# The first product of a feed-forward in seven block products instead of eight, for two batches at a time

## The chip, the cores and the metric

The kernel runs on one core of a Trainium2 chip. The metric is the device time of one execution in microseconds (us), the median of the runs shown. The engines are TensorE (PE, and PEld for its weight loads), VectorE (DVE), ScalarE (ACT), GpSimd (POOL) and the queue of SyncE (SP), which issues nearly every DMA.

## The reference

Four batches, each of 512 tokens with 512 features, pass through one block with cross attention (16 heads of 32 features):

```python
x = layer_norm(hidden_states, ln1_w, ln1_b)
q, k, v = x @ q_w + q_b, ctx @ k_w + k_b, ctx @ v_w + v_b     # split into 16 heads
out = softmax(q k^T / sqrt(32) + mask) v
hidden = out @ cproj_w + cproj_b + hidden_states
y = layer_norm(hidden, ln2_w, ln2_b)
y = gelu(y @ fc_w + fc_b)                                     # 512 -> 2048
return hidden + y @ proj_w + proj_b                           # 2048 -> 512
```

The change is to the line with `fc_w`. Everything is float32.

## The kernel before, in words

A product in float32 is formed as three passes of TensorE on `float32r` operands. Each operand is split into a high part (a rounded copy) and a low part (operand minus high part), and `mm3` (lines 487 to 489) issues high by high, low by high and high by low into one bank of PSUM. So each operand costs one copy and one subtraction of its size on some engine before TensorE can use it.

Stages: projections; attention, a loop of 64 steps i (16 head groups s, four key blocks kc each); then the feed-forward, a loop of NJ = 64 steps i, with b = i // 16 the batch and f = i % 16 the slab of 128 hidden features. `fc(i)` forms hidden features f of batch b for its 512 tokens: four blocks of 128 input features, 12 matmuls of 128x512, into bank 4 or 5. ScalarE's `gelu(i)` (line 832) reads the bank, VectorE splits the result into the tile HR (line 1178 the copy, line 1180 the subtraction), and `pj(i)` multiplies it with `proj_w`: 12 matmuls that accumulate into banks 0 to 3 through the 16 steps of a batch. TensorE's order is fc(i), pj(i-1), so that the GELU and the split of a step have a whole product to hide behind. Steps 2 to 5 also hold `cproj(3, c)`, the attention's output projection for the last batch, 12 matmuls each.

Weights are loaded once: `load_slab(f)` brings 256 KB of `fc_w` and 256 KB of `proj_w` into the raw tile RW; `slab_high` and `slab_low` (line 838 on ScalarE or 1066 on VectorE, lines 1221 or 1044 for the low part) split them, and all 16 slabs then stay in SBUF for the four batches. From step 12 on nothing of the weights is loaded or split.

The second layer norm of batch b+1 runs beside the steps of batch b: `ln2_load`, `statistics` (line 932), `aggregate`, `root` on GpSimd (line 1226), `norm` (945), a transpose through DRAM (`y_block` 960, `y_store` 345, `y_load` 352), `y_affine` (964), `y_high` on ScalarE (849) and `y_low` on GpSimd (1221). At the end of a batch VectorE adds the banks to the residual (`add`, line 1190), SP stores them (455), reloads the tile with the next batch's residual (477), and GpSimd adds the bias (1349, four instructions a batch).

Each engine works its own list in program order. A wait of one instruction holds all behind it on that engine. The order is written out by hand, engine by engine, and semaphores tie the lists together. In attention, VectorE's or GpSimd's `pair_add` (lines 1038, 1325) adds pairs of exponentials, `sums(15)` on TensorE (625) needs the last of them, and `divide_a` to `divide_c` with `split_out(15)` and `out_low(15)` lead from it to `cproj(3, c)`.

## Time and profile before

| | |
|---|---|
| median of 3 runs | 771.24 us (770.92 to 771.43) |
| the profiled execution, first to last instruction | 769.3 us |
| its own time | not given apart; the median stands 1.9 us above its span |
| granted TensorE clock | 0.999 of full |
| busy: PE, DVE, ACT, POOL | 744.1, 457.1, 281.4, 299.1 us |
| DMA | 103.25 MB, mean 134 GB/s |

A matmul's start is measured and its end is modelled, so its listed length overlaps the next one's; the pace of TensorE is read from start to start.

### The profile page before, as it was taken

The page shows a single profiled execution, that of the slowest core. Times are in us where ns is not written, and L with a number is a line of the kernel's source. Part 1 is how long each engine was busy: PE and PEld are TensorE (multiplying, and loading weights), DVE is VectorE, ACT ScalarE, POOL GpSimd, SP SyncE. Part 2 cuts the span into 40 slices and gives each one's busy share as a digit, 9 for nine tenths or more (in the row PEclk, how much of TensorE's full clock was granted, in tenths as well). Part 3 has the DMA queues.
Part 4 walks back from the last instruction along what each step waited for, and adds up shares of the span by engine and source line. Part 5 has one row for each costly group of instructions (what it writes and reads, how often), then busy time and mean ns, then how long its engine had stood idle before and what let it go on. Part 6 is the DMA issues. An engine that isn't in the chain of part 4 may idle for free.

```text
span 769.3 us, 10036 instructions
## 1 busy us (share of the span) xinstructions
PE 744.1 (97%) x3664; PEld 514.2 (67%) x3664; DVE 457.1 (59%) x995; ACT 281.4 (37%) x492; POOL 299.1 (39%) x183
## 2 busy tenths in 40 slices
PE   7999999989999999999999999999999999999998
PEld 5878886733344444444436888888888888888886
DVE  6673347778888888898697668443424333232213
ACT  4534241276766566667682011211112111211110
POOL 2654150068998778798754002212002200220000
PEclk9999999999999999999999999999999999999999
DMA  9656377597666785678641537240220413030001
GB/s 328 231 167 214 136 220 240 193 268 167 158 164 146 184 216 145 156 209 177 176 136 53 181 109 202 74 165 0 42 69 18 147 18 93 1 109 1 1 0 55
DMA packets 94385, 103.25 MB, mean 134 GB/s; under 512 B 39968, under 2 KB 48420, under 8 KB 94336
## 3 DMA queue, kind: packets, MB, share of 16 engines
q1 hardware_dynamic: 94192, 102.59, 46.5%
q8 instruction: 29, 0.48, 0.2%
q14 instruction: 20, 0.16, 0.1%
q10 hardware_dynamic: 144, 0.02, 0.0%
HBM read 73.08 MB, written 29.37 MB: 133 GB/s over the span
## 4 chain that ended last, share of the span: by engine, by line
PE 80%; DVE 12%; issue 3%; ACT 2%; DMA 1%; POOL 1%; SPq 0%; ACTq 0%; DVEq 0%
PE ps L487 22%; PE ps L488 21%; PE ps L489 21%; DVE ps L1009 6%; PE ps L594 4%; PE ps L610 4%; PE ps L579 4%; PE ps L625 3%; DVE R L1144 2%; ACT Pt L797 1%; PE ps L547 1%; DVE mx L1009 1%; DMA qs<-BIG 1%; DVE R L945 1%; DVE st L932 1%
## 5 line engine op out<-in xcount | busy, mean ns | idle before, releaser
L797 ACT ACTIVATE Pt<-ps 128x512 f32<-128x512 f32 x256 | 137.6, 598 | 70.9 <-PE ps L594 69.6
L1178 DVE CAST HR<-R 128x512 fp32r<-128x512 f32 x52 | 24.9, 478 | 186.0 <-ACT R L832 186.0
L832 ACT ACTIVATE R<-ps,cols 128x512 f32<-128x512 f32 x52 | 35.9, 690 | 227.2 <-PE ps L489 227.1
L594 PE MATMUL ps<-BIG 98*128 98x512 f32 x256 | 93.2, 439 | 3.6 <-ACT Pt L797 3.2
L1009 DVE CUSTOM_DVE_ANT_0 ps<-ps,FU 128x512 f32<-128x512 f32 x128 | 84.6, 724 | 14.9 <-PE ps L579 14.8
L1009 DVE CUSTOM_DVE_ANT_0 ps<-ps,BIG 128x512 f32<-128x512 f32 x128 | 84.6, 723 | 10.8 <-PE ps L579 10.7
L594 PEld LDWEIGHTS ps<-BIG 98*128 98x128 f32 x256 | 44.2, 187 | 68.3 <-issue 29.3
L487 PE MATMUL ps<-BIG,HR 128*128 128x512 f32 x192 | 74.8, 390 | 1.0 <-DVE HR L1180 1.0
L487 PE MATMUL ps<-YT,BIG 128*128 128x512 f32 x192 | 74.9, 390 | 0.0
L488 PE MATMUL ps<-YT,BIG 128*128 128x512 f32 x192 | 74.7, 389 | 0.0
L489 PE MATMUL ps<-BIG,HR 128*128 128x512 f32 x192 | 74.7, 389 | 0.0
L489 PE MATMUL ps<-YT,BIG 128*128 128x512 f32 x192 | 74.7, 389 | 0.0
L488 PE MATMUL ps<-BIG,HR 128*128 128x512 f32 x192 | 74.7, 389 | 0.0
L610 PE MATMUL ps<-Pt,V 128*32 128x512 f32 x512 | 68.2, 605 | 0.0
L1325 POOL TENSOR_TENSOR R<-Pt 128x1024 f32<-128x1024 f32 x20 | 47.3, 2388 | 45.9 <-ACT Pt L797 45.9
L1221 POOL TENSOR_TENSOR BIG<-R,BIG 128x512 fp32r<-128x512 f32 (+1 forms) x31 | 42.2, 1388 | 42.1 <-ACT BIG L809 22.8
L487 PE MATMUL ps<-BIG 128*128 128x512 f32 x128 | 52.8, 413 | 5.8 <-DVE BIG L1077 5.8
L1221 POOL TENSOR_TENSOR YT<-R,YT 128x512 fp32r<-128x512 f32 x12 | 15.5, 1308 | 109.1 <-ACT YT L849 109.1
L1325 POOL TENSOR_TENSOR RAWY<-Pt 128x1024 f32<-128x1024 f32 x22 | 52.0, 2385 | 4.8 <-ACT Pt L797 4.8
L488 PE MATMUL ps<-BIG 128*128 128x512 f32 x128 | 50.9, 398 | 0.0
L487 PE MATMUL ps<-BIG,WK 128*128 128x512 f32 x128 | 50.8, 397 | 0.0
L489 PE MATMUL ps<-BIG 128*128 128x512 f32 x128 | 50.7, 396 | 0.0
(132 smaller groups left out, 1371.3 us busy)
## 6 DMA issues: line engine op xcount, KB each, us to landing
BIG<-qs SPq DMA_DIRECT2D x62, 256.0 KB, 2.8
BIG<-ks SPq DMA_DIRECT2D x62, 256.0 KB, 3.2
ks<-BIG SPq DMA_DIRECT2D x32, 256.0 KB, 2.0
qs<-BIG SPq DMA_DIRECT2D x32, 256.0 KB, 5.8
R<-hd SPq DMA_DIRECT2D x28, 256.0 KB, 3.9
R<-in_x SPq DMA_DIRECT2D x16, 256.0 KB, 5.4
hd<-R SPq DMA_DIRECT2D x16, 256.0 KB, 3.2
yt<-FU SPq DMA_DIRECT2D x64, 64.0 KB, 1.9
```

The source lines that it names most:

```text
L487: eng.matmul(outp, a[0], b[0], start=first, stop=False)
L488: eng.matmul(outp, a[1], b[0], start=False, stop=False)
L489: return eng.matmul(outp, a[0], b[1], start=False, stop=last)
L579: eng.matmul(bank(bank_b(RB[("s1", 4 * group + j)])), lead(s)[r, 0, qc * 128:(qc + 1) * 128], lead(s)[r, 1, :], start=True, stop=True).the ...
L594: eng.matmul(bk, K_[0:98, j, kc * 128:(kc + 1) * 128], Q_[0:98, j, :], start=True, stop=True).then_inc(S["p_ra"], 1)
L610: ins = eng.matmul(bank(7)[32 * j:32 * j + 32, :], V[:, 4 * b + kc, c:c + 32], Pt[:, r, j % 2, :], start=kc == 0, stop=kc == 3)
L797: eng.activation(Pt[:, r, j % 2, :], bank(bank_a(("s2", i, j))), ACT.Exp, scale=SCALE).then_inc(S["a_ra"], 1)
L832: eng.activation(g, bank(4 + i % 2), ACT.Gelu_apprx_tanh, bias=fcb[:, f:f + 1]).then_inc(S["a_g"], 1)
L1009: eng.tensor_tensor_reduce(out=scores, in0=scores, in1=MASK[s // 4], scale=1.0, scalar=-3.4e38, op0=ALU.add, op1=ALU.max, accum_out=mx[:, ...
L1178: eng.tensor_copy(HR[:, n, 0, :], g).then_inc(S["v_hh"], 1)
L1221: eng.tensor_tensor(dst, src, high.bitcast(F32), ALU.subtract).then_inc(S[name], 1)
L1325: eng.tensor_tensor(pair(m)[:, 2 * hp:2 * hp + 2, :], Pt[:, (r - 2) % 6, :, :], Pt[:, r, :, :], ALU.add).then_inc(S["g_ac"], 1)
```

## The change

Take two batches, q = 0 or 1 for the pair (2q, 2q+1). Let A be `fc_w` in 2 x 2 blocks (input features halved, hidden features halved) and B the normalised input in 2 x 2 blocks (features halved, the two batches side by side). The 2 x 2 block product takes eight block products; the Winograd form of Strassen's takes seven, with four sums of blocks of A, four of B, and more additions of results. A block product for one slab index p (0 to 7, HF = 8) is `product`: two blocks of 128 input features, 6 matmuls. So a slab pair (p, p+8) for two batches takes 42 matmuls where it took 48; `pj` keeps its 12 a step.

Each pair q now has three phases. **Front** (`fc_first`, `fc_second`, p = 0 to 7): product 1 is formed and copied out by ScalarE (`copy_first`), product 2 accumulates onto it in the bank, and the GELU follows. **Rest**: products 6, 5, 7, 4, 3 for each p, in two banks; VectorE adds between them (`add_u2`, `add_u3`, `add_c22`, `add_c21`, `add_c12`), and products 7, 4 and 3 wait for `add_u2`, `add_u3` and `add_c22`. **Second product**: 32 steps `pj(n)`, back to back. The hidden features of a pair are held in SBUF (`hidden`). The sums of weight blocks are formed on GpSimd (`weight_sums`, four instructions of 128x256 into one buffer SUMS), copied on ScalarE (`rest_high`, 256 then 1024 columns) and subtracted on VectorE (`rest_low`). The sums of input blocks are formed on VectorE (`blocks`, four of 128x1024), copied on ScalarE (`block_high`, five) and subtracted on VectorE (n = 0, 1) and GpSimd (n = 2, 3, 4). Weights are loaded and split again for each pair of batches, in 112 loads of 256 KB through a ring of four. The core of the diff:

```diff
+        SUMS = FU.rearrange("p a n -> p (a n)")
...
+        RAW_W = []
+        for q in range(2):
+            RAW_W += [("wf", HF * q + p, p) for p in range(HF)]
+            for p in range(HF):
+                RAW_W += [("wr", HF * q + p, p), ("wr", HF * q + p, p + HF)]
+            RAW_W += [("pj", NF * b + f, f) for b in (2 * q, 2 * q + 1) for f in range(NF)]
...
+        def raw_done(n):
+            kind, m, _ = RAW_W[n]
+            if kind == "wf":
+                return front_low(m)
+            return ("v_wr", 2 * m + 2) if kind == "wr" else ("g_pj", m + 1)
...
+            def store_out(b):
+                for c in range(4):
+                    sp.wait_ge("v_o", 4 * b + c + 1)
+                    eng.dma_start(ov[4 * b + c], R2[:, c, :]).then_inc(S[f"d_o{c}"], 16)
...
+                            if n == 8 + c:
+                                y_store(2, c)
+                            if n == 17 + c:
+                                y_store(3, c)
+                        if n == 12:
+                            y_load(2)
+                        if n == 21:
+                            y_load(3)
+                    if n == 18:
+                        store_out(2 * q)
+                        residual(2 * q + 1)
...
+                for k in ks:
+                    ins = mm3(outp, [x[:, 128 * k:128 * k + 128] for x in a], [y[:, k - ks[0], :] for y in b],
+                              first and k == ks[0], k == ks[-1], onto=not first)
+                return ins
...
+            def fc_first(q, p):
+                m = HF * q + p
...
+                pe.wait_ge(*front_low(m))
+                pe.wait_ge("a_yp", 4 * q + 2)
+                pe.wait_ge("g_yp", 4 * q + 2)
+                product(bank(FRONT_BANKS[q][p % 4]), front(q, p), [YT0[:, h, 0:2, :] for h in range(2)], (0, 1),
+                        True).then_inc(S["p_p1"], 1)
...
+            def fc_second(q, p):
+                m = HF * q + p
...
+                product(bank(FRONT_BANKS[q][p % 4]), front(q, p), [YT0[:, h, 2:4, :] for h in range(2)], (2, 3),
+                        False).then_inc(S["p_p2"], 1)
...
+            def fc_rest(q, p, which):
+                m = HF * q + p
+                b, c = (bank(FRONT_BANKS[q][(2 * p + j) % 4]) for j in range(2))
+                outp, a, y, done = {6: (b, 2, 1, "p_p6"), 5: (c, 1, 0, "p_p5"), 7: (b, 3, 2, "p_p7"),
+                                    4: (b, 0, 3, "p_p4"), 3: (c, 4, 4, "p_p3")}[which]
+                pe.wait_ge("v_wr", 2 * m + 2)
+                pe.wait_ge("a_yq", 5 * q + y + 1)
+                pe.wait_ge(*(("v_yq", 2 * q + y + 1) if y < 2 else ("g_yq", 3 * q + y - 1)))
+                if which in (6, 5):
+                    if p < 2:
+                        pe.wait_ge("a_g11", HF * q + 5 + 2 * p + (which == 5))
+                    else:
+                        pe.wait_ge(*(("v_c21", m - 1) if which == 6 else ("v_c12", m - 1)))
+                elif which == 7:
+                    pe.wait_ge("v_u2", m + 1)
+                elif which == 4:
+                    pe.wait_ge("v_u3", m + 1)
+                else:
+                    pe.wait_ge("v_c22", m + 1)
+                product(outp, [x[:, 256 * a:256 * a + 256] for x in rest(p)], YQ[y], (0, 1),
+                        which in (6, 5)).then_inc(S[done], 1)
...
+            def pj(n):
+                b, f = divmod(n, NF)
+                sl = second(n)
+                pe.wait_ge("v_hl", n + 1)
+                pe.wait_ge("g_pj", n + 1)
...
+            for q in range(2):
+                fc_first(q, 0)
+                for p in range(HF):
+                    if p + 1 < HF:
+                        fc_first(q, p + 1)
...
+                    fc_second(q, p)
...
+                for which in (6, 5, 7):
+                    fc_rest(q, 0, which)
+                for p in range(HF):
+                    if p + 1 < HF:
+                        fc_rest(q, p + 1, 6)
+                    fc_rest(q, p, 4)
+                    if p + 1 < HF:
+                        fc_rest(q, p + 1, 5)
+                    fc_rest(q, p, 3)
+                    if p + 1 < HF:
+                        fc_rest(q, p + 1, 7)
+                for n in range(32 * q, 32 * q + 32):
+                    pj(n)
...
+            def rest_high(q, p):
+                m = HF * q + p
+                n = RAW_AT[("wr", m, p + HF)]
...
+                else:
+                    act.wait_ge("p_p2", 2 * HF)
+                    act.wait_ge("p_pr", 128)
+                hi = rest(p)[0]
+                eng.activation(hi[:, 0:256], raw_w(n)[:, 256:512], ACT.Copy).then_inc(S["a_wr"], 1)
+                act.wait_ge("g_s", 4 * m + 4)
+                eng.activation(hi[:, 256:1280], SUMS, ACT.Copy).then_inc(S["a_wr"], 1)
...
+            def second_high(n):
...
+                    act.wait_ge("p_pr", 4 * (n - 2))
+                eng.activation(second(n)[0], raw_w(at), ACT.Copy).then_inc(S["a_pj"], 1)
...
+            for q in range(2):
...
+                for p in range(HF):
+                    if p + 1 < HF:
+                        copy_first(q, p + 1)
+                    gelu11(q, p)
...
+                    if q == 0 and p == 6:
+                        for n in range(4):
+                            block_high(0, n)
+                    if p == 6 and q:
+                        rest_high(q, 0)
+                if q == 0:
+                    block_high(0, 4)
+                    rest_high(q, 0)
+                rest_high(q, 1)
+                gelu_rest(q, 0, 22)
+                rest_high(q, 2)
+                for p in range(HF):
+                    gelu_rest(q, p, 21)
+                    gelu_rest(q, p, 12)
+                    if p + 3 < HF:
+                        rest_high(q, p + 3)
+                    if p == 5:
+                        for n in range(3):
+                            second_high(32 * q + n)
+                    if p + 1 < HF:
+                        gelu_rest(q, p + 1, 22)
+                for n in range(32 * q, 32 * q + 32):
+                    if n + 3 < 32 * q + 32:
+                        second_high(n + 3)
+                    if q == 0:
+                        if n == 16:
+                            for k in range(4):
+                                y_high(2, k)
+                        if n == 26:
+                            for j in range(4):
+                                block_high(1, j)
+                            block_high(1, 4)
+                        if 28 <= n:
+                            front_high(1, n - 28)
...
+            def rest_low(q, p):
+                m = HF * q + p
+                hi, lo = rest(p)
+                dve.wait_ge("a_wr", 2 * m + 1)
+                eng.tensor_tensor(lo[:, 0:256], raw_w(RAW_AT[("wr", m, p + HF)])[:, 256:512], hi[:, 0:256].bitcast(F32),
+                                  ALU.subtract).then_inc(S["v_wr"], 1)
+                dve.wait_ge("a_wr", 2 * m + 2)
+                eng.tensor_tensor(lo[:, 256:1280], SUMS, hi[:, 256:1280].bitcast(F32), ALU.subtract).then_inc(S["v_wr"], 1)
...
+                for n, a, b in ((0, b2[:, 0:2, :], b1[:, 0:2, :]), (1, b2[:, 2:4, :], formed(q, 0)),
+                                (2, b2[:, 2:4, :], b2[:, 0:2, :]), (3, b1[:, 2:4, :], formed(q, 1))):
+                    if n in (1, 3):
+                        dve.wait_ge("v_tt", 4 * q + (1 if n == 1 else 2))
+                    eng.tensor_tensor(formed(q, n), a, b, ALU.subtract).then_inc(S["v_tt"], 1)
...
+            def add_u2(q, p):
...
+            def add_u3(q, p):
+                m = HF * q + p
...
+                eng.tensor_tensor(hidden(1, p + HF), bank(FRONT_BANKS[q][2 * p % 4]), hidden(0, p + HF), ALU.add).then_inc(S["v_u3"], 1)
...
+            for q in range(2):
+                for p in range(HF):
...
+                    if q == 0 and p == 5:
+                        blocks(0)
+                    if q == 0 and p == 6:
+                        block_low(0, 0)
+                        block_low(0, 1)
+                rest_low(q, 0)
+                add_u2(q, 0)
+                rest_low(q, 1)
+                add_u3(q, 0)
+                add_c22(q, 0)
+                for p in range(HF):
+                    if p + 1 < HF:
+                        add_u2(q, p + 1)
+                    add_c21(q, p)
+                    add_c12(q, p)
+                    if p + 2 < HF:
+                        rest_low(q, p + 2)
+                    if p + 1 < HF:
+                        add_u3(q, p + 1)
+                        add_c22(q, p + 1)
+                    if p >= HF - 2:
+                        split_hidden(32 * q + p - HF + 2)
+                for n in range(32):
+                    m = 32 * q + n
+                    if n >= 2:
+                        split_hidden(m)
+                    if n == 17:
+                        add_out(2 * q)
+                    if q == 0:
...
+                            if n - at == 7:
+                                for c in range(4):
+                                    norm(LN[b], b % 2, 4 + b, c)
...
+                            if 14 <= n - at < 16:
+                                for k in (2 * (n - at) - 28, 2 * (n - at) - 27):
+                                    y_affine(b, k)
+                        if n == 25:
+                            blocks(1)
+                        if n == 27:
+                            block_low(1, 0)
+                            block_low(1, 1)
+                        if 28 <= n:
+                            front_low_part(1, n - 28)
...
+            def block_low(q, n):
...
+            def weight_sums(q, p):
...
+                pool.wait_ge(*raw_come(n1))
...
+                a1, a2 = raw_w(n1), raw_w(n2)
+                s1, s2, s3, s4 = (SUMS[:, 256 * j:256 * j + 256] for j in range(4))
+                eng.tensor_tensor(s1, a2[:, 0:256], a2[:, 256:512], ALU.add).then_inc(S["g_s"], 1)
+                eng.tensor_tensor(s3, a1[:, 0:256], a2[:, 0:256], ALU.subtract).then_inc(S["g_s"], 1)
+                pool.wait_ge("g_s", 4 * m + 1)
+                eng.tensor_tensor(s2, s1, a1[:, 0:256], ALU.subtract).then_inc(S["g_s"], 1)
+                pool.wait_ge("g_s", 4 * m + 3)
+                eng.tensor_tensor(s4, a1[:, 256:512], s2, ALU.subtract).then_inc(S["g_s"], 1)
...
+            def second_low(n):
+                pool.wait_ge("a_pj", n + 1)
...
+            def bias_add(b):
+                pool.wait_ge("d_pb", 16)
+                for c in range(4):
+                    pool.wait_ge(f"d_hb{c}", 16 * (b + 1))
+                    eng.tensor_tensor(R2[:, c, :], R2[:, c, :], cbt[:, :], ALU.add).then_inc(S["g_hb"], 1)
...
+            for q in range(2):
+                weight_sums(q, 0)
+                if q == 0:
+                    for n in (2, 3, 4):
+                        block_low(0, n)
+                else:
+                    bias_add(2)
+                for p in range(HF):
+                    if p + 1 < HF:
+                        weight_sums(q, p + 1)
+                    if q == 0 and p == 2:
+                        bias_add(0)
+                    if p == HF - 1:
+                        for n in range(3):
+                            second_low(32 * q + n)
+                for n in range(32):
+                    m = 32 * q + n
+                    if n + 3 < 32:
+                        second_low(m + 3)
+                    if n == 21:
+                        bias_add(2 * q + 1)
+                    if q == 0:
+                        if n == 6:
+                            root(0, 6)
+                        if n == 15:
+                            root(1, 7)
+                        if n == 17:
+                            for k in range(4):
+                                y_low(2, k)
+                        if n == 27:
+                            for j in (2, 3, 4):
+                                block_low(1, j)
```

## Rows read from the trace of the kernel before

**Rows 1.** The page: busy time, share of the span and instructions by engine.
```profile
PE 744.1 (97%) x3664; PEld 514.2 (67%) x3664; DVE 457.1 (59%) x995; ACT 281.4 (37%) x492; POOL 299.1 (39%) x183
```

**Rows 2.** Feed-forward, windows: us; busy PE, PEld, DVE, ACT, POOL; clock, DMA share, GB/s.
```profile
403.30:764.80 361.50, 360.47 (x1596) 296.81 (x1597) 152.97 (x270) 54.24 (x81) 49.55 (x37) 1.00 0.23 68
```

**Rows 3.** PE's timeline: start, length, line, form [idle before <-releaser].
```profile
417.52 0.50 PE L487 MATMUL ps<-BIG,HR 128*128 128x512 f32 x1 [1.03 <-DVE HR L1180]
...
420.39 0.39 PE L487 MATMUL ps<-BIG 128*128 128x512 f32 x1
...
431.27 0.39 PE L487 MATMUL ps<-YT,BIG 128*128 128x512 f32 x1
```

**Rows 4.** Groups from 420 us on: xcount | busy us, mean ns of one.
```profile
L1180 DVE TENSOR_TENSOR HR<-R,HR 128x512 fp32r<-128x512 f32 x52 | 38.0, 730 | 1.8
L832 ACT ACTIVATE R<-ps,cols 128x512 f32<-128x512 f32 x52 | 35.9, 690 | 227.2 <-PE ps L489 227.1
...
L1178 DVE CAST HR<-R 128x512 fp32r<-128x512 f32 x52 | 24.9, 478 | 186.0 <-ACT R L832 186.0
L1349 POOL TENSOR_TENSOR R<-R,cbt 128x512 f32<-128x512 f32 x16 | 21.7, 1387 | 64.8 <-DMA R<-hd 64.8
...
L1190 DVE TENSOR_TENSOR R<-ps,R 128x512 f32<-128x512 f32 x16 | 10.2, 684 | 1.5 <-PE ps L489 1.5
...
L945 DVE TENSOR_SCALAR R<-R,mv,rs 128x512 f32<-128x512 f32 x12 | 6.5, 541 | 0.0
```

**Rows 5.** Groups of ACT over the whole run.
```profile
L757 ACT ACTIVATE BIG<-RAWY 128x1024 fp32r<-128x1024 f32 x4 | 4.0, 1049 | 0.0
```

**Rows 6.** Groups of POOL over the whole run.
```profile
L1221 POOL TENSOR_TENSOR BIG<-R,BIG 128x512 fp32r<-128x512 f32 x29 | 37.5, 1316 | 28.3 <-ACT BIG L809 22.8 <-ACT BIG L763 5.5
...
L1221 POOL TENSOR_TENSOR BIG<-RAWY,BIG 128x1024 fp32r<-128x1024 f32 x4 | 9.7, 2448 | 18.1 <-ACT BIG L757 18.1
...
L1226 POOL TENSOR_TENSOR rs<-ve,mh 128x4 f32<-128x4 f32 x8 | 8.5, 1059 | 74.1 <-DVE ve L941 74.1
```

**Rows 7.** Line 1038, DVE's sums of 128x1024: duration ns min/median/max.
```profile
L1038 DVE TENSOR_TENSOR V<-Pt x6: 1212/2068/2301, 378.7 to 402.9; 128x1024 f32<-128x1024 f32 x6
```

**Rows 8.** DVE's timeline.
```profile
389.40 4.52 DVE L1038 TENSOR_TENSOR V<-Pt 128x1024 f32<-128x1024 f32 x2
...
401.20 2.90 DVE L1038 TENSOR_TENSOR V<-Pt 128x1024 f32<-128x1024 f32 x2 [0.45 <-ACT Pt L797]
...
473.00 1.27 DVE L1178 CAST HR<-HN 128x512 fp32r<-128x512 f32 x1 [1.21 <-ACT HN L832]
```

**Rows 9.** POOL's timeline.
```profile
389.07 8.21 POOL L1221 TENSOR_TENSOR YT<-HN,YT 128x512 fp32r<-128x512 f32 x4 [1.47 <-ACT YT L849]
...
471.44 5.69 POOL L1349 TENSOR_TENSOR R<-R,cbt 128x512 f32<-128x512 f32 x4 [18.54 <-DMA R<-hd]
```

**Rows 10.** DMA issues: xcount, KB each, median us from issue to landing.
```profile
yt<-FU SPq DMA_DIRECT2D x64, 64.0 KB, 1.9
RW<-in_fc_w SPq DMA_DIRECT2D x16, 256.0 KB, 3.3
...
R<-yt SPq DMA_DIRECT2D x12, 256.0 KB, 4.2
```

**Rows 11.** SP's timeline: the time its queue takes to issue.
```profile
480.07 1.75 SPq L352 DMA_DIRECT2D R<-yt  x4
...
764.71 2.37 SPq L455 DMA_DIRECT2D out<-R  x4
```

**Rows 12.** PE's first matmuls.
```profile
5.75 0.76 PE L487 MATMUL ps<-BIG 128*128 128x512 f32 x1 [5.75 <-DVE BIG L1077]
...
9.73 0.63 PE L487 MATMUL ps<-BIG 128*128 128x512 f32 x1
...
10.77 0.39 PE L487 MATMUL ps<-BIG 128*128 128x512 f32 x1
```

**Rows 13.** The stretch after the last matmul, in the columns of rows 2.
```profile
766.00:769.00 3.00, 0.00 (x0) 0.00 (x0) 0.73 (x2) 0.00 (x0) 0.00 (x0) 0.87 0.78 292
```

586 lines of the change are left out of this document (358 added, 228 removed).

## The prediction

> **What bounds the kernel now.** I read the page first, for busy shares: TensorE is busy 744.1 of 769.3 us, the others under 60% [rows 1]. Then the view of windows, cut to the feed-forward: PE 360.47 of 361.50 us, while DVE works 153.0, ACT 54.2, POOL 49.6 [rows 2]. So TensorE alone sets this stage's end, and every matmul taken out there is worth its time as long as nothing else makes TensorE wait. Then PE's own timeline, for the pace and the gaps: from 420.39 to 431.27 us it starts 48 matmuls, 10.88/48 = 0.2267 us each, and the only gap in the stage is 1.03 us at its start [rows 3]. The listed 0.39 us are not the pace. A step of 12 matmuls is 2.72 us, a block product of 6 is 1.36 us.
>
> The sum is made against the profiled span of 769.3 us; the median of the runs, 771.24, stands 1.9 above it, and I carry that over. A measurement of this kernel can tell about 0.2%, 1.5 us, from no change.
>
> **What is removed.** 64 x 12 = 768 first-product matmuls become 16 x 42 = 672. 96 x 0.2267 = **-21.8 us**, all of it on the path.
>
> **What is added** is work for engines that had room on average, placed where TensorE may have to wait for it. The durations: a split of a hidden tile on DVE is a copy of 0.41 and a subtraction of 0.69 alone, means 0.48 and 0.73; a GELU 0.69; a PSUM addition 0.68; a bias addition on POOL 1.39; one `norm` 0.54 [rows 4]. A copy of 128x1024 on ACT is 1.05 [rows 5]. On POOL 128x512 is 1.32 and 128x1024 is 2.45, so 1.13 for 512 columns; 128x256 isn't in the trace, its bounds are the smallest instruction, 1.06, and a line through the two, 0.75 [rows 6]. I take 0.75, since 256 columns lie on that line, and keep the other for the range. DVE's 128x1024 sum is 1.21 alone [rows 7]; its 128x256 I put at 0.4 by the same reasoning.
>
> **DVE and POOL together.** DVE's 128x1024 sums at 389.4 take 2.26 each, not 1.21, while POOL's four subtractions beside them take 2.05 each, not 1.3 [rows 8, 9]. At 473.0 copy and subtraction take 1.27 and 1.67 beside POOL's bias additions [rows 8, 9]. Each engine seems to wait for the other's instruction to end. That speaks against this change, which puts POOL beside DVE throughout. The Trainium skill says so (SBUF — State Buffer, Who interferes with whom): the second port pair is an exclusive lock, held for a whole instruction, taken by a DVE instruction with two SBUF inputs or in a two-port mode. Under that rule every DVE split queues behind a POOL instruction; without it DVE's durations would stay at the short ones. The trace agrees with the rule.
>
> *Start of the stage, q = 0.* Four `statistics` and the aggregates go ahead of the last pair sums on DVE, some 2.5 to 3 us, where it had 0.45 us to spare [rows 8]; the removed `slab_high(2)`/`slab_low(2)` came only after those. `cproj(3,0)` then waits for the quotient's chain through ACT and POOL. The gap of 1.03 us goes [rows 3]. Between 0 and 3 net, I take **+1**.
>
> *Front to rest, q = 0.* Product 6 needs `block_high`, `rest_high(0)` and `rest_low(0)`. ACT's list puts four blocks behind GELU 6 and a fifth behind GELU 7. From the end of `fc_second(6)`: 0.69 + 4 x 1.05 + 0.69 + 1.05 + 0.3 + 1.05 on ACT, then 1.21 on DVE = 9.2 us. TensorE has one product, 1.36, to do meanwhile: 7.8 us idle. POOL's three `block_low` of 2.45 lie there too, the last one just ahead of DVE's `rest_low`, which costs up to 2.5 more. After the start, 6(1) needs the chain again: sums 4 x 0.75, copy 1.05, subtraction 1.21 = 5.3 us against three products, 4.1: 1.2 more. 9 to 13, I take **+11.5**.
>
> *Front to rest, q = 1.* `rest_high` waits for the last front product (its buffer overlays `front`): 0.3 + 1.05 + 1.21 + 0.2 = 2.8, and the same 1.2. **+4** (3 to 5).
>
> *The clock.* After 5.75 us without work TensorE's first matmuls start 0.427 us apart until about 10.5 us, then 0.227 (rates of 1.2 and 2.4 GHz) [rows 12]; and in the 3 us after the last matmul the granted clock averages 0.87 [rows 13]. So the idle 11 us should drop the clock: 11 matmuls x 0.2 = 2.2 us, partly inside the 1.2 above. **+1** (0 to 4).
>
> *Rest, steady.* Five products are 6.80 us. But a loop closes through DVE: `add_c12`, `rest_low(p+2)` (0.3 + 1.13 by spacing), `add_u3`, then products 4, 5, 3: 0.19 (from a product's last start plus 0.23 to its modelled end, and to DVE's start) + 0.6 + 0.3 + 1.13 + 0.69 + 0.05 + 4.2 = 7.16. 0.36 x 14 = **+5** (0 to 8, the top if POOL's sums take 1.06). `bias_add(0)` stands among them: 4 x 1.39 on POOL, beside `rest_low`: **+1.5** (0 to 2.5). The two loads of the next slab, 3.3 us to landing [rows 10], have a period of 7; covered.
>
> *Second product, q = 0.* The period is 2.72; a split has 1.6 us of slack. (a) n = 7 and 14 to 18: `norm` x4, affine x4, `add_out` (2.7) and `y_low` x4 pile up on DVE and POOL: 0 if they don't share, 4.7 if they do. (b) SP, n = 17 to 21: four stores (2.37), the residual's wait and loads, the transposes' stores (2.0 each), then `y_load(3)` (1.75 to issue, 4.2 to land) [rows 10, 11]: `y_affine(3)`, ahead of the split of n = 24 on DVE, starts 3.3 to 5 us late, and the raw `proj_w` tiles come late too. (c) n = 25: `blocks(1)`, 4 x 1.13 after a split of 1.1, against 2.72 + 1.6: 2.1 to 4.6. (d) n = 27: DVE's `block_low` waits for ACT's `block_high(1,0)`, which waits for `pj(26)`'s end; the split of n = 28 stands behind: 0.65 + 2 x 1.05 + 1.2 + 1.1 = 5.1 against 2.72: 2.5. (e) POOL does three `block_low` (7.3) before the low part for n = 31: ready 15.8 us after `pj(26)` against 13.4: 2.4, and 5.1 with DVE's splits in between. Together 10.3 to 21.9, I take **+14.5**. *q = 1* has only the bias additions at n = 21: **+1** (0.3 to 1.8).
>
> *Costed at nothing:* the front's copies and GELUs (1.9 of 2.72 us on ACT), the low parts of `proj_w` (POOL 1.3 of 2.72), the 112 loads (one of 256 KB in 2.72 us is 96 GB/s, below the run's mean of 134). Their cover is TensorE's own period; if it were gone, POOL's 64 low parts would be the next thing late.
>
> Sum: -21.8 + 1 + 11.5 + 4 + 1 + 5 + 1.5 + 14.5 + 1 = **+17.7**; 771.2 + 17.7 = **789.0**.
>
> **Rivals.** (R1) DVE and POOL don't disturb each other much and the side work fits: the low ends, 0 + 9 + 3 + 0 + 3 + 0 + 10.3 + 0.3 = 25.6, less 21.8: 775. Against it stand [rows 8, 9]. (R2) Faster. Its place is the second product of q = 0: if DVE's and SP's extra work there costs under 5 us rather than 14.5, and the steady rest nothing, 11.5 + 4 + 1 + 2 = 18.5 against 21.8: 768. It decides at 21.8 us of TensorE waits in all. For it: DVE is idle over half of this stage [rows 2], and one late split is soon made up. Against it: the two hand-overs alone take some 13 of it. (R3) The chain POOL, ACT, DVE sets the rest's period: POOL's sums at 1.06 to 1.32 each make 4.2 to 5.3 + 2.3 + waits = 7.5 to 8, 0.5 more for 14 periods and 2 more at each hand-over: 800. (R4) Terms cancel within 1.5 us.
>
> **How the numbers follow.** Forecast, 780 to 797: 0.57. R1: 0.13. R2: 0.13. R3: 0.12. R4: 0.05. So faster 0.13, same 0.05, slower 0.82. The range leaves out R2 and R4's lower half and the far end of R3: 773 to 802; the forecast's own terms, all at their ends, give 772 to 804.
>
> **What would show it.** Right: 96 matmuls fewer at an unchanged 0.227 us; a PE gap of 8 to 12 us before the first product 6 of q = 0, ended by DVE's `rest_low`, and of about 3 for q = 1; starts 0.427 apart behind the long gap; rest periods near 7.2; DVE splits of 1.2 to 3 us beside POOL's instructions; gaps in the second product of q = 0 ended by the split or by POOL's low part. Wrong: a stage without PE gaps of several us; a matmul pace that changes; DVE's durations as short as alone; or the second product of q = 0 at 32 x 2.72 = 87 us.

## The result: 831.6 us, 60 above the kernel before

The changed kernel takes 831.62 us (median of 4, 830.73 to 833.20) against 771.34 (770.92 to 771.72) for the kernel before in the same session: a ratio of 1.0786, 95% interval 1.0772 to 1.0799. Slower, as forecast, but by 60 us where I had 18, and 30 us above the top of my range. The profiled spans are 831.4 and 769.3 us, so 62 us are to be found.

The page of the kernel after, its busy shares, and the strips of 40 slices of PE and of the clock:

```profile
span 831.4 us, 10419 instructions
PE 747.7 (90%) x3568; PEld 505.1 (61%) x3568; DVE 546.7 (66%) x1077; ACT 362.2 (44%) x618; POOL 448.3 (54%) x307
PE   7999999989999999999995888987775988899998
PEclk9999999999999999999997999989977989999999
```

The matmuls are 96 fewer, yet PE is busier than before [rows 1], 747.7 for 744.1: some of what is left ran slower. PE's strip is broken from the 22nd slice on, and only there does the clock's strip fall to 7 or 8, in five slices. The view of windows, cut at the stages (columns as in [rows 2]; the last three figures are the granted clock, the DMA share and GB/s):

```profile
430.00:450.00 20.00, 10.94 (x46) 8.71 (x45) 15.09 (x14) 9.44 (x13) 13.65 (x7) 0.82 0.57 170
450.00:520.00 70.00, 61.28 (x248) 47.86 (x247) 41.29 (x58) 26.97 (x40) 30.21 (x36) 0.95 0.32 102
520.00:620.00 100.00, 79.95 (x314) 62.90 (x313) 69.50 (x103) 18.52 (x30) 52.85 (x36) 0.90 0.47 132
620.00:650.00 30.00, 20.64 (x75) 16.11 (x75) 15.64 (x18) 9.31 (x13) 11.35 (x6) 0.82 0.30 96
650.00:720.00 70.00, 62.77 (x259) 49.73 (x258) 31.64 (x46) 31.32 (x49) 26.11 (x34) 0.95 0.25 76
720.00:831.00 111.00, 104.39 (x454) 84.42 (x452) 57.33 (x87) 27.14 (x42) 58.20 (x40) 1.00 0.34 105
```

Before, PE was busy nearly all of this stage [rows 2]. Now no engine is full in the broken windows: DVE, the busiest beside PE, has 15.1 of 20 us in the first and 69.5 of 100 us in the third. PE waits, for work that is late rather than for an engine that is full. The waits, from PE's timeline (distances of two starts less 0.227 us): hand-over of the first half 9.22 and 1.36; steady rest 13 of 1.05 or 0.94 and one of 2.43; its second product 4.54, 4.26, 6.73, 3.08, 2.84, 6.85 and three smaller ones (0.68, 0.39, 1.48), 30.9 in all; hand-over of the second half 2.91; its second product 2.5. With 2.7 at the stage's start that is 65.5 us. Besides, 78 matmuls in nine stretches, each behind a wait of 2.43 us or more, start late after the one before them, nearly all 0.427 us instead of 0.227 (the first of a stretch often 0.59): 16.6 us more than at 0.227.

**The hand-over.** PE's timeline around the longest wait; the bracket names the idle time and what ended it:

```profile
439.54 0.39 PE L590 MATMUL ps<-YT,RX 128*128 128x512 f32 x1
448.99 0.80 PE L588 MATMUL ps<-SLX,BIG 128*128 128x512 f32 x1 [9.06 <-DVE BIG L1322]
449.58 0.63 PE L589 MATMUL ps<-SLX,BIG 128*128 128x512 f32 x1
```

And what DVE, POOL and ACT did before it, from their timelines:

```profile
440.81 2.34 DVE L1339 TENSOR_TENSOR SLX<-BF,SLX 128x1024 fp32r<-128x1024 f32 x2
...
445.88 3.06 DVE L1322 TENSOR_TENSOR BIG<-FU,BIG 128x1024 fp32r<-128x1024 f32 x1 [0.23 <-ACT BIG L1047]
445.33 5.82 POOL L1595 TENSOR_TENSOR YT<-BF,YT 128x1024 fp32r<-128x1024 f32 x2
444.80 1.05 ACT L1047 ACTIVATE BIG<-FU 128x1024 fp32r<-128x1024 f32 x1
```

`rest_low` (L1322) takes 3.06 us, 1.21 alone, beside POOL's `block_low` (L1595). It starts when ACT's copy (L1047) is done, at 445.8; so of the 9.2 us of waiting about 1.9 are the stretching, and the rest is the way to that copy.

**The rest, steady.** DVE's, ACT's and PE's timelines at the start of one product 6:

```profile
489.11 0.69 DVE L1381 TENSOR_TENSOR BF<-ps,BF 128x512 f32<-128x512 f32 x1 [2.03 <-PE ps L590]
489.72 0.42 DVE L1319 TENSOR_TENSOR BIG<-RW,BIG 128x256 fp32r<-128x256 f32 x1
490.05 1.22 DVE L1322 TENSOR_TENSOR BIG<-FU,BIG 128x1024 fp32r<-128x1024 f32 x1
486.43 1.06 ACT L1047 ACTIVATE BIG<-FU 128x1024 fp32r<-128x1024 f32 x1 [3.55 <-POOL FU L1661]
491.32 0.50 PE L588 MATMUL ps<-SLX,BIG 128*128 128x512 f32 x1 [0.90 <-DVE BIG L1322]
```

ACT had the high part ready at 487.49. DVE waited for product 3 to do `add_c12` first (L1381), then `rest_low(p+2)`, and PE, which has only product 7 to do meanwhile, waited for that: 0.2 + 0.6 + 0.3 + 1.2 = 2.3 us against 1.36, so some 1.0; 1.05 came.

**The second product of the first half.** Three of its waits, each with what DVE or POOL did (timelines; L1391 and L1393 are the copy and the subtraction of the split, L1214 is `norm`, L1600 `root`, L1233 `y_affine`, L1672 `bias_add`, L1595 at 630.78 and 633.10 `block_low`, L1313 `front_low`):

```profile
539.31 1.02 POOL L1600 TENSOR_TENSOR rs<-ve,mh 128x4 f32<-128x4 f32 x1
540.36 2.87 DVE L1214 TENSOR_SCALAR HN<-HN,mv,rs 128x512 f32<-128x512 f32 x4 [4.57 <-POOL rs L1600]
544.35 0.79 PE L588 MATMUL ps<-BIG,HR 128*128 128x512 f32 x1 [4.38 <-DVE HR L1393]
...
598.53 5.31 POOL L1672 TENSOR_TENSOR R<-R,cbt 128x512 f32<-128x512 f32 x4
600.71 2.02 DVE L1233 TENSOR_SCALAR R<-R,cols 128x512 f32<-128x512 f32 x2 [4.48 <-DMA R<-yt]
602.64 1.48 DVE L1391 CAST HR<-BF 128x512 fp32r<-128x512 f32 x1
604.16 1.64 DVE L1393 TENSOR_TENSOR HR<-BF,HR 128x512 fp32r<-128x512 f32 x1
605.85 0.79 PE L588 MATMUL ps<-BIG,HR 128*128 128x512 f32 x1 [6.57 <-DVE HR L1393]
...
630.78 2.35 POOL L1595 TENSOR_TENSOR YT<-BF,YT 128x1024 fp32r<-128x1024 f32 x1
633.10 2.78 POOL L1595 TENSOR_TENSOR YT<-R,YT 128x1024 fp32r<-128x1024 f32 x1
632.48 1.20 DVE L1313 TENSOR_TENSOR RX<-RW,RX 128x512 fp32r<-128x512 f32 x1 [5.94 <-ACT RX L1031]
633.60 2.56 DVE L1391 CAST HR<-BF 128x512 fp32r<-128x512 f32 x1
636.20 1.63 DVE L1393 TENSOR_TENSOR HR<-BF,HR 128x512 fp32r<-128x512 f32 x1
637.88 0.79 PE L588 MATMUL ps<-BIG,HR 128*128 128x512 f32 x1 [6.68 <-DVE HR L1393]
```

All three read alike: DVE is idle for 4.5 to 6 us, since the next instruction of its list, a piece of work for the next half, still waits, and the split that PE needs stands behind it. In the second and the third the split itself is stretched as well, beside POOL's `bias_add` and then its `block_low`: by 3.1 us in the third (2.56 and 1.63 for 0.41 and 0.69 alone).

### The profile page after: what moved, and what is told of

Read it like the earlier page. It is cut to its first block, busy times and chain, and to the rows that moved or that the text cites. A ratio compares the mean times of both kernels' runs of the same rounds, so it can differ in the third digit from the quotient of the medians.

```text
span 831.4 us, 10419 instructions
## 1 busy us (share of the span) xinstructions
PE 747.7 (90%) x3568; PEld 505.1 (61%) x3568; DVE 546.7 (66%) x1077; ACT 362.2 (44%) x618; POOL 448.3 (54%) x307
## 4 chain that ended last, share of the span: by engine, by line
PE 67%; DVE 19%; issue 4%; POOL 4%; ACT 3%; DMA 2%; SPq 2%; ACTq 0%; DVEq 0%
PE ps L588 18%; PE ps L590 17%; PE ps L589 17%; DVE ps L1278 5%; PE ps L711 4%; PE ps L695 4%; PE ps L680 3%; PE ps L726 3%; DVE BIG L1322 2%; DVE R L1481 2%; DVE R L1214 1%; POOL BIG L1595 1%; DVE HR L1391 1%; SPq L410 1%; DVE BF L1381 1%
## 5 line engine op out<-in xcount | busy, mean ns | idle before, releaser
L1595 POOL TENSOR_TENSOR BIG<-RW,BIG 128x512 fp32r<-128x512 f32 x66 | 101.5, 1542 | 112.7 <-ACT BIG L1057 110.9
L588 PE MATMUL ps<-BIG,HR 128*128 128x512 f32 x256 | 105.7, 413 | 31.5 <-DVE HR L1393 28.8
L1057 ACT ACTIVATE BIG<-RW 128x512 fp32r<-128x512 f32 x64 | 40.2, 631 | 154.8 <-PE ps L590 135.1
L590 PE MATMUL ps<-BIG,HR 128*128 128x512 f32 x256 | 103.5, 404 | 0.0
L589 PE MATMUL ps<-BIG,HR 128*128 128x512 f32 x256 | 103.3, 404 | 0.0
L588 PEld LDWEIGHTS ps<-BIG,HR 128*128 128x128 f32 x256 | 50.6, 198 | 47.4 <-DVE HR L1393 33.4
L1391 DVE CAST HR<-BF 128x512 fp32r<-128x512 f32 x64 | 37.2, 582 | 55.9 <-PE ps L590 55.8
L1595 POOL TENSOR_TENSOR BIG<-R,BIG 128x512 fp32r<-128x512 f32 (+1 forms) x31 | 42.4, 1395 | 43.5 <-ACT BIG L968 24.4
L588 PE MATMUL ps<-SLX,BIG 128*128 128x512 f32 x96 | 41.7, 435 | 25.1 <-DVE BIG L1322 25.1
L1656 POOL TENSOR_TENSOR FU<-RW 128x256 f32<-128x256 f32 x16 | 11.8, 740 | 95.9 <-DVE BIG L1322 59.5
L588 PE MATMUL ps<-BIG 128*128 128x512 f32 x128 | 52.7, 412 | 6.1 <-DVE BIG L1410 5.8
L589 PEld LDWEIGHTS ps<-BIG,HR 128*128 128x128 f32 x256 | 50.9, 199 | 10.5
L590 PEld LDWEIGHTS ps<-BIG,HR 128*128 128x128 f32 x256 | 50.2, 196 | 11.2
L1393 DVE TENSOR_TENSOR HR<-BF,HR 128x512 fp32r<-128x512 f32 x64 | 53.9, 843 | 2.2
```

What stands on the lines that cost most here:

```text
L588: eng.matmul(outp, a[0], b[0], start=first, stop=False, skip_group_check=onto)
L589: eng.matmul(outp, a[1], b[0], start=False, stop=False, skip_group_check=onto)
L590: return eng.matmul(outp, a[0], b[1], start=False, stop=last, skip_group_check=onto)
L1057: eng.activation(second(n)[0], raw_w(at), ACT.Copy).then_inc(S["a_pj"], 1)
L1391: eng.tensor_copy(HR[:, n % 2, 0, :], g).then_inc(S["v_hh"], 1)
L1393: eng.tensor_tensor(HR[:, n % 2, 1, :], g, HR[:, n % 2, 0, :].bitcast(F32), ALU.subtract).then_inc(S["v_hl"], 1)
```

## The experiments

The theory after this: the saving of 21.8 us is real and in full; against it stand waits of PE, each made by the place of one piece of side work in a list, and each long one brings slow matmuls. The rivals to it: the clock (a cause of its own), POOL's weight sums (the chain POOL, ACT, DVE as the rest's bound), and port time of DVE and POOL together, so that gaps would only move.

**1. `rest_low` ahead of `add_c12` (e1_low_before_c12).**

```diff
                     add_c21(q, p)
-                    add_c12(q, p)
                     if p + 2 < HF:
                         rest_low(q, p + 2)
+                    add_c12(q, p)
```

> The changed kernel (831.6 us) with one pair of instructions moved on VectorE: in the rest phase rest_low(p+2) stands ahead of add_c12(p). Theory: the 13 PE gaps of 0.94 to 1.06 us, one a period, are there because product 6 of the next slab waits for rest_low, which waits in VectorE's list for product 3; they close, and with restarts 13 to 16 us go: 816 to 819. Rival: the chain of GpSimd's sums, ScalarE's copy and VectorE's subtraction sets the period of 7.99 us; then at most 3 us go: 828 or more.

Measured: 816.55 us (811.95 to 817.46), ratio 1.0577 (1.0548 to 1.0607), 15.1 less than the change. The same window of the steady rest, first in the kernel after, then here:

```profile
453.00:506.00 53.00, 45.96 (x189) 36.00 (x188) 30.90 (x43) 20.65 (x31) 23.36 (x30) 0.97 0.20 60
```

```profile
453.00:506.00 53.00, 51.73 (x223) 41.97 (x223) 37.24 (x52) 25.30 (x38) 27.95 (x32) 0.99 0.38 121
```

34 matmuls more in the same 53 us: all waits of 1.05 are gone, and so is the one of 2.43; one of 0.94 at the end of each rest stays. The time is the one expected (816 to 819). POOL's sums were not the bound.

**2. `root` one step earlier, ahead of `second_low` (e2_root_first).**

```diff
+                    if q == 0:
+                        if n == 5:
+                            root(0, 6)
+                        if n == 14:
+                            root(1, 7)
                     if n + 3 < 32:
                         second_low(m + 3)
...
                     if q == 0:
-                        if n == 6:
-                            root(0, 6)
-                        if n == 15:
-                            root(1, 7)
```

> The changed kernel with root(0,6) and root(1,7) on GpSimd one step earlier and ahead of second_low instead of behind it. Theory: the gaps of 4.54 and 4.26 us near 540 and 572 us come from norm waiting for root, which stands behind a second_low that waits for the end of a later pj; they close, and the slow matmuls behind them go too (2.2 + 1.6 us): 818 to 821. Rival: the norms stretched beside GpSimd (2.87 us for four) are what makes the split late; then the gaps keep 3 us or more each: 826 or more.

Measured: 824.73 us (822.18 to 826.55), ratio 1.0693. The waits of 4.54 and 4.26 shrink to about 1 each, so the cause is right; but only 7 us come, where 11 to 14 were expected: in the profile a later wait (6.85) grows to 8.44, another (3.08) to 3.84, and the hand-over's stands at 11.11, for 9.22. The edit does not touch that last one, so it scatters by some 2 us between runs.

**3. `rest_high(1,0)` one step earlier (e3_rest_high_early).** It now waits for the last user of its own buffer only.

```diff
-                    if p == 6 and q:
+                    if p == 5 and q:
                         rest_high(q, 0)
...
+                elif p == 0:
+                    act.wait_ge("p_p3", HF)
                 else:
                     act.wait_ge("p_p2", 2 * HF)
                     act.wait_ge("p_pr", 128)
```

> The changed kernel with rest_high(1,0) one step earlier on ScalarE and without its wait for the end of the front phase, since its buffer lies beside the front's. Theory: the gap of 2.91 us near 670 us goes, with the 13 slow matmuls behind it (2.6 us): 825 to 827. Rival: product 6 of slab 1 then waits as long, since its own chain starts late: 829 or more.

Measured: 829.32 us (828.95 to 830.75), ratio 1.0758. The wait of 2.91 at 669 us and its slow matmuls, 2.96, are gone, yet the time falls by 2.3, where 5 to 7 were expected and the rival had 3 at most. In the profile the rest of the second half has one more wait of 1.05, at 675 us, for slab 1, as the rival said, though far shorter than it had it; and the untouched first hand-over took 11.0 for 9.2.

**4. The price of a wait alone (gap5, gap2).** The kernel before, with PE made to wait six times, for five or for two small POOL instructions in a row; no other work changes.

```diff
+                if i in GAPS:
+                    pe.wait_ge("g_x", 5 * (GAPS.index(i) + 1))
```

(This is gap5; gap2 has 2 in place of 5.)

> The kernel before (771.3 us) with six waits put into TensorE's list, at steps 50, 52 and so on to 60: behind fc(i) it waits until GpSimd, which starts at fc(i)'s end, has done five instructions of 128x4 one after the other (about 1.0 us each by line 1226, so gaps near 5.3 us). If an idle stretch costs only itself: 6 x 5.3 = 32 us more, 803. If the clock falls in each and stays low for 8 to 10 matmuls, as behind the gaps of the changed kernel: 6 x (5.3 + 2.0) = 44, 815.

> As gap5, but two instructions on GpSimd per wait instead of five. By gap5's profile (6.24 us of gap for five, 1.24 each) the gaps are near 2.5 us: 15 us more than 771.1 if the clock holds (786), 29 more (800) if it falls behind each one.

Measured: gap5 823.75 us, ratio 1.0672 (1.0655 to 1.0690), 52.7 more than before; gap2 801.55, ratio 1.0383 (1.0349 to 1.0417), 30.6 more. PE's timeline of gap5 at its first wait, then of gap2 at its own:

```profile
697.15 0.80 PE L488 MATMUL ps<-BIG,HR 128*128 128x512 f32 x1 [6.08 <-POOL mx L1359]
697.74 0.63 PE L489 MATMUL ps<-BIG,HR 128*128 128x512 f32 x1
```

```profile
693.07 0.50 PE L488 MATMUL ps<-BIG,HR 128*128 128x512 f32 x1 [2.83 <-POOL mx L1359]
693.41 0.39 PE L489 MATMUL ps<-BIG,HR 128*128 128x512 f32 x1
...
694.67 0.63 PE L488 MATMUL ps<-BIG,HR 128*128 128x512 f32 x1
695.10 0.63 PE L489 MATMUL ps<-BIG,HR 128*128 128x512 f32 x1
```

In gap5 six waits of 6.24 (5.3 was expected) are 37.4, and 66 slow matmuls behind them cost 14.1: 51.5 of 52.7. In gap2 six of 2.98 are 17.9, and 55 slow matmuls 11.6: 29.5 of 30.6. So in these two runs a wait costs its length and some 2 us more, 1.4 to 3.0, whether it lasts 3 or 6 us. Nothing else was changed, so waits alone are enough to bring slow matmuls, and those of the changed kernel, each stretch behind a wait, need no cause of their own. Not every wait near 3 us brings them, though: behind 2.61 us in e2_root_first, and 2.90 in all1 and 2.92 in e5_second_spread (both below), the matmuls went on 0.23 us apart. PE's timeline of e5_second_spread:

```profile
656.72 0.50 PE L588 MATMUL ps<-SLX,BIG 128*128 128x512 f32 x1 [2.76 <-DVE BIG L1319]
657.05 0.39 PE L589 MATMUL ps<-SLX,BIG 128*128 128x512 f32 x1
657.29 0.40 PE L590 MATMUL ps<-SLX,BIG 128*128 128x512 f32 x1
```

**5. The order at the first hand-over (e4_handover).** ACT: `block_high(0,0)` a step earlier, `rest_high(0,0)` between blocks 1 and 2; POOL: `weight_sums(0,1)` between its `block_low` 2 and 3.

> The changed kernel with the hand-over from front to rest of q = 0 in another order: ScalarE does block_high(0,0) one step earlier, then block_high(0,1), rest_high(0,0) and block_high(0,2) ahead of the last GELU, and the other two blocks behind it; GpSimd does weight_sums(0,1) ahead of its last two block_low. Theory: rest_low(0) ends 4 to 6 us earlier, the gap of 9 to 11 us falls to 3.5 to 6 and the wait before product 6 of slab 1 grows to 2 to 3: 825 to 828. The clock still falls in the gap. Rival: the gap is set by GpSimd's and VectorE's turns with each other, not by ScalarE's list; then under 2 us go.

Measured: 832.13 us (828.63 to 835.34), ratio 1.0794: nothing. The first wait shrinks from 9.2 to 7.8, the next grows from 1.4 to 3.4 and now has slow matmuls of its own. ACT's copy was now ready at 441.0 instead of 445.8, and the first `rest_low` was not stretched either. DVE's timeline shows what bound instead:

```profile
441.08 4.50 DVE L1342 TENSOR_TENSOR SLX<-BF,SLX 128x1024 fp32r<-128x1024 f32 x2
...
445.83 1.21 DVE L1325 TENSOR_TENSOR BIG<-FU,BIG 128x1024 fp32r<-128x1024 f32 x1
```

That is DVE's own order: its two `block_low` (L1342), 4.50 us beside POOL's for 2.34 before, stand ahead of `rest_low`. The second `rest_low`, with POOL's last two `block_low` beside it, took 2.09 and 3.36, and that is the wait of 3.4.

**6. Side work spread out (e5_second_spread, on top of 2).** One `norm`, `y_high`, `y_low`, `blocks` and `block_low` a step instead of four at once; `bias_add(0)`, which stood in the rest, a row a step in the second product, those of batches 1 and 2 moved to the second half, that of batch 3 a row a step; SP's store and residual at n = 22 instead of 18, and `store_out(1)` and `add_out(1)` to step 3 of the second half's front.

> The changed kernel with the side work of q = 0's second product spread, one piece a step: root as in e2_root_first, norm, y_low, blocks and the block splits one a step, the bias additions of batches 0 and 3 one a step and of batches 1 and 2 moved to later, and SP's store_out(0) and residual(1) behind y_load(3). Theory: the gaps between 539 and 638 us (30.9 us in sum) with their slow matmuls (8 us) come from pieces in a lump ahead of a split; all but 5 us of them and the bias gap of 2.4 go: 831.6 - 33 = 795 to 802. Rival: GpSimd and VectorE together have no room there, whatever the order (GpSimd is busy 52.9 and VectorE 69.5 of 100 us); then at least 15 us of gaps stay: 810 or more.

Measured: 817.23 us (816.16 to 817.86), ratio 1.0599. That is above the 795 to 802 expected, and by its number in the rival's range. Up to 585 us the bundled waits become nine of 0.65 to 1.5 us, with hardly a slow matmul; but waits of 3.9 and 8.8 stay in its last steps. The count of instructions on DVE and POOL is the same over the run, so in those steps it was the bundling that made the long waits; the last steps this run does not settle.

**7. All five together (all1).**

> All edits of e1 to e5 together. Theory (the waits are separate, each closed by its own edit, and the clock falls only in gaps of over 2.4 us): 831.6 - 15 (e1) - 33 (e5 with e2) - 2.3 to 5 (e3) - 5 (e4) = 774 to 778, near the kernel before (771). If it falls under 771, the seven products pay once the waits are out. Rival: waits close only to open elsewhere: 785 or more.

Measured: 797.00 us (795.89 to 798.88), ratio 1.0341 (1.0325 to 1.0357): 34.6 off, some 20 less than hoped, and so in the range of the rival, that waits open elsewhere. 9.5 us of waits stand at the hand-over, and 8.88 at the end of the second product, where DVE's `front_low(1,0)` waits for ACT's `front_high(1,0)`, itself behind `second_high(31)`, which needs PE to go on.

**8. The order made again (all2).**

```diff
-                        if 28 <= n:
-                            front_low_part(1, n - 28)
+                        if n == 31:
+                            for p in range(4):
+                                front_low_part(1, p)
...
-                    for n in (2, 3, 4):
-                        block_low(0, n)
+                    weight_sums(0, 1)
+                    block_low(0, 4)
+                    block_low(0, 3)
```

(The first is DVE's list, the second POOL's; the rest is in the expectation. It isn't order alone: the `norm`s go to ACT and one `block_low` from POOL to DVE.)

> Everything of the run all1 except its order at the hand-over, and besides: (a) the second product of the first half: the four lows of the second half's front weights (0.68 each) stand behind the last split on DVE, so that no split waits for ACT's front_high; the norms of batches 2 and 3 (8 x 0.54 to 1.6) are made on ACT; bias_add(0) is spread over four rest periods; store_out(0) and residual(1) on SP stand five steps apart. (b) the hand-over of the first half: the second weight load of the first rest column goes out ahead of the y transpose's load, so POOL's weight sums can start some 5 us earlier; DVE makes three blocks, then block_low(1), rest_low(0), block_low(0) and block_low(2), and POOL makes weight_sums(1) ahead of its two block_lows, so that no POOL work lies beside rest_low(0). Theory (the time above the saving of 21.8 us is PE gaps made by the placing of side work, each gap above some 2.5 us with about 2 us of slow clock behind it): from all1's 797.0 the gaps of 8.88 (+2.36 slow), 2.69 (+1.51), 1.91, about 6.5 us of the gaps of 0.7, and 7 of the 9.5 at the hand-over (+1.96) go: 765 to 770. Rival 1, that the work is bound by the shared port of DVE and POOL and gaps only move: 785 or more, with the sum of gaps beyond 20 us. Rival 2, that the hand-over's chain is set by data (the y transpose lands at 431), not by order: a gap of 5 us or more stays there, 772 to 776.

Measured: 782.10 us (781.57 to 782.74), ratio 1.0137 (1.0114 to 1.0159). The time lies between the theory's 770 and the first rival's 785, above what the second had. The 8.88 is gone, the hand-over stands at 5.6 (1.19 and 4.42). But where POOL's `block_low` went, behind n = 28, waits of 2.47 and 3.29 came with a CAST of 2.57 and a subtraction of 2.73 on DVE: there the first rival was right, time of DVE and POOL beside each other had only moved.

**9. POOL's work beside DVE taken out (all3).** `weight_sums(0,1)`, all `block_low(0,·)` and `y_low(2)` on DVE, blocks 2 and 3 of the second half into its front, POOL's `block_low(1,·)` behind DVE's last split.

> On top of all2. Second product of the first half: y_low(2) moves from POOL to DVE (4 x 0.68 for 4 x 1.3 to 1.7), the block_lows 2 to 4 of the second half go out on POOL only behind the last split and its front lows, blocks 2 and 3 and block_lows 0 and 1 stand in the second half's front on DVE, statistics of batch 3 one step earlier, add_out(0) behind the y transposes. Hand-over of the first half: all five block_lows and weight_sums(1) on DVE (1.2 and about 1.3 instead of 2.4 and 2.9 on POOL), the front lows 5 to 7 and the second rest load ahead of the y transpose's waits. Theory (DVE and POOL take turns at two-input work in SBUF, so what counts is the sum of their port time in each period, and PE gaps are what exceeds the period): from all2's 782.1 some 12 of the 15 us of gaps and slow clock at 535 to 607 go, and about 4 of the 7.4 at the hand-over: 766 to 769, under the kernel before. Rival (DVE alone is too full: its 1.21 for a split and what stands beside it, whatever POOL does): the gaps of 0.4 to 0.9 stay, 774 to 778. Rival 2 (the second half's first GELUs wait for the late block_lows and PE stops for the banks): a gap of 3 us or more at 610 to 625.

Measured: 778.75 us (777.49 to 779.21), ratio 1.0096 (1.0080 to 1.0113). Not the 766 to 769 expected. The hand-over falls to 1.08, 0.97, 0.34, 1.04 and 0.54, the second product to four waits of 0.45 to 0.60 before its end. But a new one of 11.19 stands at 599.7, from an order of mine: DVE's `add_out(1)` waited for POOL's `bias_add(1)`, with the next `front_low` behind it. DVE's timeline:

```profile
592.56 1.22 DVE L1363 TENSOR_TENSOR BF<-HN,BF 128x1024 f32<-128x1024 f32 x1
606.05 0.69 DVE L1446 TENSOR_TENSOR R<-ps,R 128x512 f32<-128x512 f32 x1 [12.27 <-POOL R L1743]
```

**10. That order mended (all4), and one thing put back (e6_y_low_on_pool).**

```diff
-                    if q and p == 3:
-                        add_out(1)
...
                     if q and p >= 4:
                         front_low_part(1, p)
+                    if q and p == 7:
+                        add_out(1)
...
+                    bias_add(1)
                     for j in (2, 3, 4):
                         block_low(1, j)
-                    bias_add(1)
```

> On top of all3, whose largest gap (11.19 us at 599.7, and 2.74 of slow clock behind it) came of an order of mine: DVE's add_out(1) at step 3 of the second half's front waited for POOL's bias_add(1), which stood behind three block_lows, and the front lows 4 to 7 stood behind add_out(1). Here bias_add(1) goes ahead of the block_lows, add_out(1) and SP's store_out(1) go behind the front. Theory: the gap and its slow stretch go whole, 778.75 - 13.9 = 765, from 763.5 to 767, under the kernel before (771); the remaining gaps are those of 0.4 to 1.1 us. Rival: the second half's GELUs then wait for the late block_lows, and a gap of some us comes back between 600 and 625: 768 or more.

> all4 with one thing put back: the four y_low(2) (128x512, two operands in SBUF) on POOL in the second product's steps 17 to 20 instead of on DVE in steps 25 and 27. DVE has 2.7 us less work, POOL 5.2 to 5.9 more. Theory (the two engines take turns at such work, so DVE's splits are stretched by what POOL does beside them): four gaps of 0.6 to 0.8 us at 550 to 570, 2.5 to 4 us slower than all4. Rival (DVE's own sum is what fills the period): the same as all4 or up to 2 us faster, since the gaps of 0.45 to 0.5 at 572 to 579 go and none comes.

Measured: all4 766.52 us (764.65 to 766.77) against 770.78, ratio 0.9939 (0.9927 to 0.9952): **4.3 us under the kernel before**, as expected (763.5 to 767). The page of all4, and its windows of the first hand-over and second product:

```profile
span 762.8 us, 10426 instructions
PE 729.9 (96%) x3568; PEld 494.1 (65%) x3568; DVE 559.0 (73%) x1082; ACT 368.3 (48%) x626; POOL 436.2 (57%) x296
PEclk9999999999999999999999999999999999999999
```

```profile
430.00:450.00 20.00, 18.35 (x78) 13.94 (x77) 18.62 (x24) 11.71 (x16) 3.68 (x3) 1.00 0.38 121
520.00:590.00 70.00, 68.32 (x294) 54.32 (x293) 59.47 (x87) 23.68 (x38) 37.96 (x25) 1.00 0.70 189
```

The clock is at its full level throughout, no wait in the feed-forward is longer than 1.21 us, and PE's busy time has fallen by 14.2 us where the page of before had 744.1 [rows 1]. The 21.8 us are not all had: 16 waits of 0.3 to 1.2 us remain, 10.6 us in all, and another 5 us lie in single starts 0.30 to 0.51 us apart, for which this profile names no wait.

e6 took 764.96 us (764.75 to 766.13), ratio 0.9927 (0.9914 to 0.9941), no different from all4; the theory had wanted 2.5 to 4 us more. DVE's and POOL's timelines there:

```profile
558.82 1.67 DVE L1440 TENSOR_TENSOR HR<-BF,HR 128x512 fp32r<-128x512 f32 x1
558.37 1.56 POOL L1661 TENSOR_TENSOR BIG<-RW,BIG 128x512 fp32r<-128x512 f32 x1
559.90 1.74 POOL L1661 TENSOR_TENSOR YT<-HN,YT 128x512 fp32r<-128x512 f32 x1
```

The stretching is there, 1.67 for 0.69. That agrees with the Trainium skill (SBUF — State Buffer, Who interferes with whom), by which a DVE instruction with two inputs in SBUF contends with a POOL instruction that reads SBUF. But DVE's tiles start further apart than the period of 2.72 in only one longer row, five from 551.3 us on, 2.9 to 3.7 us, and PE's longest wait there is 0.42: I take it that the lead that the splits had took the rest. Read so, a stretched instruction costs only what the period and the lead cannot take.

## Why the prediction was wrong, step by step

- **Removed, -21.8: right.** 3568 matmuls, and in undisturbed stretches the pace of [rows 3].
- **Start, +1: inside its range (0 to 3), not by the way given.** 0.94 and 0.44 stand for the one gap of before, 1.19 by the same measure: 0.2 more. The wait named, of `cproj(3,0)` for the quotient, did not come; the two were ended by DVE's `front_low` and by a low part on POOL.
- **Hand-over of the first half, +11.5: right.** 9.22 + 1.36 = 10.6 (9 to 13), ended by `rest_low` beside POOL's `block_low`, as written. Other runs with the same order there had 11.0 and 11.1 for the 9.2.
- **Hand-over of the second half, +4 (3 to 5): slightly too high.** 2.91, by the wait named; the second wait did not come. The reason I gave was wrong: the first slab's buffer doesn't overlay the front's, only the code waited as if it did, and e3 takes the wait out.
- **The clock, +1 (0 to 4): wrong, the term was mis-sized: it measured 16.6.** I gave it to the one gap of 11 us. In this kernel slow matmuls follow every wait of 2.43 us or more, nine stretches of 1.4 to 3.0 us each; gap2 and gap5 show the same with nothing else changed. I had [rows 12] and [rows 13], only long idle times, and none of the short waits that my own other terms were about to make.
- **Rest, steady, +5: wrong, the wrong loop.** 15.9 together with `bias_add`, which I had at 1.5 and which is the 2.43. I closed the loop through `rest_low(p+2)`, `add_u3` and products 4, 5 and 3, which gives 0.36. The shorter loop was missed: product 6(p+2) itself waits for `rest_low(p+2)`, which stands behind `add_c12(p)`, with one product of 1.36 as cover; 1.05. e1 shows it: the order alone takes them away, all but the last of each half.
- **Second product of the first half, +14.5: wrong, the term was mis-sized: it measured 30.9.** (a) had `norm`s and their stretching, 0 to 4.7, and left out the wait in front of them: `root` stood behind `second_low(n+3)` on POOL, which needs PE's next step, 4.54 and 4.26. e2 shows it. (b), 3.3 to 5, gave 6.73: the DMA's wait as written, then cast and subtraction stretched to 1.48 and 1.64. (c) 3.08, inside 2.1 to 4.6. (d) 2.84 for 2.5, right. (e) had POOL's three `block_low`, up to 5.1, and their part is there, 3.1 us in the stretched split; what I left out is DVE's `front_low(1,0)` behind ACT's `front_high(1,0)`, whose own cost is small, and with it the wait is 6.85. all2, which moves it, loses that wait.
- **Second product of the second half, +1:** 2.5.

The waits sum to 65.5 and the slow matmuls to 16.6; less the 21.8, and less the 2.6 us of gaps that before had in this stage too, that is 58 of 62. Of the other 4, about 2.5 are the 23 or so restarts outside the slow stretches, whose first matmul takes about 0.34 to the next and not 0.227; I didn't test that.

The working has slips of its own. The terms' upper ends add up to 59.2, less the 21.8 that is 809 and not 804. R1 calls 3 the low end of the steady rest, whose stated low end is 0. Under (c), 4 x 1.13 + 1.1 is only 1.3 above 2.72 + 1.6, or 2.4 with the next split, so the 2.1 to 4.6 isn't derived; the 15.8 and 13.4 of (e) aren't either. None of them makes up the miss: even the 809 is 23 short.

The rivals: R3 was refuted by e1, and R1 by the stretched rows. R4, that the terms cancel, was far off. R2, that waits stay under 21.8, was wrong for this kernel but not impossible: all4 is there, with the same products, another order, and some side work on other engines.

## What to carry to other kernels

For each instruction that a fast engine waits for, write down everything ahead of it in its engine's list and what each of those waits for, and count the product that covers it; a small instruction of the next stage, set ahead of a needed one, costs its wait and not its length. When TensorE is the bound, price each wait of about 3 us or more at its length plus some 2 us of slow matmuls (between 2.4 and 3 us they came or did not), and prefer many waits under 1.5 us to one of 5. Before a saving of arithmetic is given up for its side work, that work's order is worth another look, and so is which engine does it: here the same products cost 60 us in one arrangement and gave 4 in another. How much of the 65 us between is order alone isn't separated; e1, e2 and e5 changed only the order and took off 15, 7 and (with e2's) 14 us, while all2 and all3 also moved work from POOL to DVE and from DVE to ACT.

## What the runs showed of the hardware that I had not expected

- After the first wait of 2.98 us in gap2 PE went on at its full pace until 694.34, and was slow from 694.67 to 697.66; the fourth was like it, and after the other four, as after all six of 6.24 us, it was slow from the start. Yet the sums are near each other, 11.6 and 14.1 for six. Behind waits of 2.61, 2.90 and 2.92 us in three other runs nothing was slow, and behind one of 2.41 us it was in e3_rest_high_early and not in e4_handover. Behind waits of up to 1.9 us no slow stretch began in any of these runs, and all4, with no wait above 1.21, had a granted clock of 1.00 throughout.
- The length of a slow stretch scattered from 6 to 14 matmuls behind waits of one length, 2.98 us.
- POOL's 128x256 sum took 0.73 us alone, DVE's 0.42, and four of them on DVE (all3) 1.5 in all, 440.11 to 441.66, where POOL in the changed kernel had taken 3.0, 451.12 to 454.11.
